# Attention matmuls cut into four column tiles, two jobs of VectorE handed to ScalarE and GpSimd, and a new hand-written order

## What is computed

```python
xn = _layernorm(x, axis=-1)
q, k, v = split_heads(xn @ W_q), split_heads(xn @ W_k), split_heads(xn @ W_v)
q, k = _apply_rope(q, cos, sin), _apply_rope(k, cos, sin)
scores = einsum('bhqd,bhkd->bhqk', q, k);  scores = where(causal, -inf, scores)
attn = softmax(scores / sqrt(hd), axis=-1)
s = einsum('bhqk,bhkd->bhqd', attn, v) ... @ W_o
g = _silu(_L0_ffn_ref(xn, w_router, w_fc, w_proj))
x = x + s * g
```

## Time and profile before

| | |
|---|---|
| median of three runs | 2545.77 us |
| the profiled execution | 2543.15 us |
| its span in the profile | 2541.4 us |
| TensorE matmul busy | 2411.2 us, 95% |
| TensorE weight loads busy | 1227.6 us, 48% |
| VectorE busy | 2100.8 us, 83% |
| ScalarE busy | 1732.6 us, 68% |
| GpSimd busy | 969.9 us, 38% |
| granted TensorE clock over the span | 0.981 |

### The profile page before, as it was taken

One profiled execution on the slowest core, in us unless ns is written; L12 is line 12 of the kernel. 1 busy time (PEld: TensorE's weight loads), 2 busy tenths in 40 slices (PEclk: granted clock), 3 DMA queues, 4 the chain that ended last, 5 costly groups with the idle time before them and its releaser, 6 DMA issues. The chain is left out here.

```text
span 2541.4 us, 51444 instructions
## 1 busy us (share of the span) xinstructions
PE 2411.2 (95%) x16364; PEld 1227.6 (48%) x16365; DVE 2100.8 (83%) x5995; ACT 1732.6 (68%) x4063; POOL 969.9 (38%) x1124
## 2 busy tenths in 40 slices
PE   7979985999999999999999999999999999899887
PEld 6767761334334334333333333333433433588676
DVE  7979988989989989988998998998998999355344
ACT  6767771777777777777777777777777777555211
POOL 6979994112122222222222222222222222222676
PEclk9999995999999999999999999999999999999999
DMA  6898977767755655655666665565565561498898
GB/s 223 276 282 284 294 260 141 156 159 147 153 93 94 116 97 90 114 102 96 104 107 128 102 110 94 99 110 100 93 106 106 92 104 44 141 311 312 266 370 273
DMA packets 302398, 403.44 MB, mean 159 GB/s; under 512 B 99248, under 2 KB 233648, under 8 KB 302000
## 3 DMA queue, kind: packets, MB, share of 16 engines
q1 hardware_dynamic: 289840, 366.58, 60.9%
q0 software_dynamic: 12288, 33.57, 4.9%
HBM read 225.46 MB, written 173.02 MB: 157 GB/s over the span
## 5 line engine op out<-in xcount | busy, mean ns | idle before, releaser
L945 DVE CUSTOM_DVE_ANT_0 dump<-ps_rows,mask 128x128 bf16<-128x128 f32 (+7 forms) x2048 | 1483.0, 755 | 171.0 <-issue 151.2
L924 ACT ACTIVATE probs<-ps_cols 128x512 f32<-128x512 f32 (+3 forms) x3072 | 1275.1, 505 | 471.6 <-PE ps_cols L1091 466.0
L1091 PE MATMUL ps_cols<-q_st,k_st 99*128 99x512 bf16 (+3 forms) x3072 | 835.6, 329 | 8.3 <-DMA q_st<-max_T 3.2
L903 POOL TENSOR_SCALAR_AFFINE_SELECT probs<-probs 128x512 f32<-128x512 f32 x512 | 325.3, 635 | 1284.9 <-ACT probs L924 1284.7
L1036 PE MATMUL ps_rows<-k_st,q_st 96*128 96x512 bf16 (+3 forms) x3072 | 776.2, 330 | 14.3 <-DVE row_max L945 6.8
L1068 PE MATMUL ps_ctx<-probs,v_st 128*32 128x512 f32 (+3 forms) x6144 | 615.5, 495 | 0.0
L1091 PEld LDWEIGHTS ps_cols<-q_st,k_st 99*128 99x128 bf16 x3072 | 274.0, 97 | 497.6 <-ACT probs L924 293.3
L1036 PEld LDWEIGHTS ps_rows<-k_st,q_st 96*128 96x128 bf16 x3072 | 279.2, 98 | 321.3 <-DVE row_max L945 168.1
L1068 PEld LDWEIGHTS ps_ctx<-probs,v_st 128*32 128x32 f32 x6144 | 140.3, 108 | 214.4 <-ACT probs L924 78.0
L945 DVE DVE_READ_ACCUMULATOR2_ANT row_max<- 128x1 f32 x2048 | 171.1, 84 | 0.2
L316 POOL TENSOR_TENSOR rest<-roped,parts 128x1024 f32<-128x1024 f32 x64 | 138.3, 2161 | 36.1 <-ACT parts L367 31.4
(11 more groups left out here) (114 smaller groups left out, 2458.6 us busy)
## 6 DMA issues: line engine op xcount, KB each, us to landing
parts_dram<-parts SPq DMA_DIRECT2D x64, 768.0 KB, 4.1
q_st<-parts_dram SPq DMA_DIRECT2D x384, 128.0 KB
k_st<-parts_dram SPq DMA_DIRECT2D x384, 128.0 KB
xs_dram<-zeros SPq DMA_DIRECT2D x36, 512.0 KB, 7.0
xs_sb<-xs_dram SPq DMA_DIRECT2D x72, 256.0 KB, 4.7
g_dram<-g_sb SPq DMA_DIRECT2D x72, 256.0 KB, 3.6
v_dram<-v_sb SPq DMA_DIRECT2D x32, 544.0 KB, 5.0
v_st<-v_dram SPq DMA_DIRECT2D x64, 272.0 KB
```

The source lines that it names most:

```text
L903: nc.gpsimd.affine_select(out=tri, in_=tri, compare_op=ALU.is_ge, fill=0.0, base=0, pattern=[[0, GH], [1, P]], channel_multiplier=-1).then ...
L924: nc.scalar.activation(probs[:, k % PB, h, 0:w], ps_cols[(GH * k + h) % CB][:, 0:w], ACT.Exp).then_inc(exp_done, 1)
L945: nc.vector.tensor_tensor_reduce(out=dump[:, even, 0:n], in0=ps_rows[:, 512 * bank:512 * bank + n], in1=mask[:, S - n:S], scale=1.0, scala ...
L1091: nc.tensor.matmul(ps_cols[(GH * k + h) % CB][:, 0:w], k_st[r][:, j // IB, h * 512 + (j % IB) * P:h * 512 + (j % IB + 1) * P], q_st[r][:, ...
```

## The change

1. Every matmul of the attention is issued in column tiles of 32. A row or column matmul of 128 stationary columns becomes four of 32 that stream the same moving operand. The transpose of maxima becomes two (32 and 16 columns). The transpose of contexts becomes plain fp32 matmuls against the 68 used columns of the identity, four tiles for each of four blocks. Only the last one of a set signals.
2. The maxima leave their bank by ScalarE (`move_max`). The contexts leave theirs by ScalarE too, into a new SBUF tile `ctx_T` (`move_ctx`). VectorE takes the reciprocals from there (`invert`), three row items later, and GpSimd multiplies (`normalise`), two steps after the transpose.
3. `slot_done` is split into `rows_done`, `max_moved`, `ctx_moved` and `normalised`. `place()` works out for each use of a bank which of them to wait for.
4. `ITEMS` and `ORDER` are new, SyncE loads the next group's maxima before it stores the contexts of half 0, and the first group's operands are loaded at tile 10 of the first phase in place of 8.

```diff
-    FIRST_GROUP_AT = 8
+    FIRST_GROUP_AT = 10
...
-        ("RR", "", "RRR", "VR"),
-        ("", "RM", "RX", ""),
-        ("RVR", "RR", "RR", ""),
-        ("R", "VR", "", ""),
-        ("R", "", "R", "VVR"),
-        ("", "", "R", "R"),
-        ("V", "R", "", "R"),
-        ("", "RV", "", "R"),
-        ("X", "M", "R", ""),
-        ("R", "", "RV", ""),
-        ("R", "R", "VV", ""),
-        ("RR", "", "", "VV"),
+        ("R", "RR", "RR", "VR"),
+        ("", "RRM", "RV", "R"),
+        ("", "RRX", "RR", ""),
+        ("VR", "", "R", "R"),
+        ("", "", "RV", "V"),
+        ("", "R", "RV", "R"),
+        ("", "R", "", "RV"),
+        ("R", "", "R", "V"),
+        ("R", "", "X", "MR"),
+        ("", "V", "R", ""),
+        ("R", "VR", "", "R"),
+        ("V", "", "", "RV"),
...
-            store_ctx(n, b, r, 0)
             if not last:
                 load_max(n + 1, (r + 1) % RING, 0)
+            store_ctx(n, b, r, 0)
...
+        def normalise(n, c):
+            pool.wait_ge(inv_ready, 2 * n + c + 1)
+            if n > 0:
+                pool.wait_ge(ctx_stored[c], 16 * n)
+            nc.gpsimd.tensor_tensor(ctx_out[:, c].rearrange("p i (h e) -> p (i h) e", h=GH), ctx_T[:, c, :, 0:HD],
+                                    inv_sum[:, c, :].unsqueeze(2).broadcast_to((P, IB * GH, HD)),
+                                    ALU.mult).then_inc(normalised, 1)
+
         def group(n, r, first, last):
             for k, (c, j, q0, w, diag_before, diag) in enumerate(STEPS):
+                for k0, _, (what, arg) in in_group(n):
+                    if what == "ctx" and k == min(k0 + 2, NS - 1):
+                        normalise(n - arg, arg)
...
+        def move_max(n, c, slot, bank):
+            act.wait_ge(slot_ready, slot + 1)
+            if n > 0:
+                act.wait_ge(max_loaded[c], 16 * n)
+            nc.scalar.activation(max_T[:, c, :], small_bank(bank)[0:PARTS * GH * IB, 0:P],
+                                 ACT.Copy).then_inc(max_moved, 1)
+
+        def move_ctx(n, c, slot, bank):
+            act.wait_ge(slot_ready, slot + 1)
+            if n > 0:
+                act.wait_ge(normalised, 2 * (n - 1) + c + 1)
+            nc.scalar.activation(ctx_T[:, c].rearrange("p i e -> p (i e)"),
+                                 ps_rows[:, 512 * bank:512 * bank + IB * GH * VP], ACT.Copy).then_inc(ctx_moved, 1)
...
-        def copy_max(m, c, slot, bank):
-
-            if not (isinstance(m, int) and m == 0):
-                dve.wait_ge(max_loaded[c], 16 * m)
-            dve.wait_ge(slot_ready, slot + 1)
-            nc.vector.tensor_copy(max_T[:, c, :], small_bank(bank)[0:PARTS * GH * IB, 0:P])\
-                .then_inc(slot_done, 1)
...
+        def invert(m, c):
+            dve.wait_ge(ctx_moved, 2 * m + c + 1)
+            if m > 0:
+                dve.wait_ge(normalised, 2 * (m - 1) + c + 1)
+            nc.vector.reciprocal(inv_sum[:, c, :], ctx_T[:, c, :, HD]).then_inc(inv_ready, 1)
...
-                mm = nc.tensor.matmul(ps_rows[:, 512 * (bank + c):512 * (bank + c) + w], q,
-                                      k_st[r][0:KS, c, h * 512:h * 512 + w], start=True, stop=True)
+                for a in range(0, P, VW):
+                    mm = nc.tensor.matmul(ps_rows[a:a + VW, 512 * (bank + c):512 * (bank + c) + w],
+                                          q_st[r][0:KS, i // IB, q0 + a:q0 + a + VW],
+                                          k_st[r][0:KS, c, h * 512:h * 512 + w], start=True, stop=True,
+                                          tile_position=(0, a))
...
+            for a in range(0, PARTS * GH * IB, VW):
+                b = min(a + VW, PARTS * GH * IB)
+                mm = nc.tensor.transpose(small_bank(bank)[a:b, 0:P], parts[:, a:b], ident_b[:], tile_position=(0, a))
...
+            used = ident_f[:].rearrange("p (h e) -> p h e", h=GH)[:, :, 0:VP]
             for i in range(IB):
-                mm = nc.tensor.transpose(ps_rows[:, 512 * bank + i * P:512 * bank + (i + 1) * P],
-                                         ctx_raw[:, c, i * P:(i + 1) * P], ident_f[:])
+                at = 512 * bank + i * GH * VP
+                for a in range(0, P, VW):
+                    mm = nc.tensor.matmul(ps_rows[a:a + VW, at:at + GH * VP].rearrange("p (h e) -> p h e", h=GH),
+                                          ctx_raw[:, c, i * P + a:i * P + a + VW], used, start=True, stop=True,
+                                          tile_position=(0, a))
...
+                    k0 = h * 512 + (j % IB) * P
+                    for a in range(0, P, VW):
+                        mm = nc.tensor.matmul(ps_cols[(GH * k + h) % CB][a:a + VW, 0:w],
+                                              k_st[r][:, j // IB, k0 + a:k0 + a + VW],
+                                              q_st[r][:, c, h * 512 + q0 - 512 * c:(h + 1) * 512],
+                                              start=True, stop=True, tile_position=(0, a))
```

More of the change, by code:

```diff
@@ L711, in attention_phase, with in_group, happens @@
     EVENTS = events()
[L712 to L734, removed]
-    def place():
[L739 to L743, removed]
+    assert not any(x in "MX" for x in ORDER[-1][-1])
+    def in_group(n):
+        return [(k, h, what) for k, h, what in EVENTS if what[0] != "values" and happens(what, n)]
+    def happens(what, n):
+        return not (n == 0 and what in (("ctx", 1), ("values", -1)) or
+                    n == N - 1 and (what[0] == "row" or what == ("max", 0)))
+    def place():
+        uses = [[("row", t) for t in range(NI)] + [("max", 0)]] + \
+               [[what for _, _, what in in_group(n)] for n in range(N)] + [[("ctx", 1)]]
+        out, last, number = [], {}, 0
+        left = {"row": 0, "max": 0, "ctx": 0}
+        for whats in uses:
+            pos, placed = 0, {}
             for what in whats:
@@ L747, in place, with moves_after, rows_before_inverse @@
                 banks = [(pos + i) % RB for i in range(2 if wide else 1)]
-                last_use = max(used.get(x, -1) for x in banks)
-                placed.append((banks[0], at - last_use if last_use >= 0 else None))
-                used.update({x: at for x in banks})
+                before = {"row": 0, "max": 0, "ctx": 0}
+                for kind, count in [last[b] for b in banks if b in last]:
+                    before[kind] = max(before[kind], count)
+                left[what[0]] += 1
+                last.update({b: (what[0], left[what[0]]) for b in banks})
+                placed[what] = (number, banks[0], before)
                 pos += len(banks)
-                at += 1
+                number += 1
             out.append(placed)
[L754 to L764, removed]
+        return out
+    FIRST_ROWS, *PLACES = place()
     def small_bank(i):
         return ps_rows[:, 512 * i:512 * (i + 1)].bitcast(BF16)
-    assert PER % 2 == 0 and (GH * NS) % CB == 0 and NS % PB == 0
+    def moves_after(n, k, h):
+        k0, h0 = (k, h - 1) if h > 0 else (k - 1, GH - 1)
+        return [what for kk, hh, what in in_group(n) if (kk, hh) == (k0, h0) and what[0] != "row"]
+    INVERT_AFTER = 3
+    def rows_before_inverse(n):
+        out, rows, due = {}, 0, {}
+        place_of = [(k, h) for k, h, _ in in_group(n)]
+        for i, (k, h, what) in enumerate(in_group(n)):
+            if what[0] == "row":
+                rows += 1
+            elif what[0] == "ctx":
+                same = sum(1 for x, y in zip(place_of[i + 1:], in_group(n)[i + 1:]) if x == (k, h) and y[2][0] == "row")
+                out[what] = min(rows + same + INVERT_AFTER, NI)
+        return out
+    assert (GH * NS) % CB == 0 and NS % PB == 0
     def groups(eng, body):
@@ L999, in group @@
             if last:
                 for i in range(MAX_OPS):
[L1001 to L1017 removed]
+                    split_max(n, 1, i)
+            else:
+                for t in range(NI):
+                    row_item(n + 1, t, *PLACES[n]["row", t][:2])
+                    if t < MAX_OPS:
+                        split_max(n, 1, t)
+                    if HALF_ITEMS <= t < HALF_ITEMS + MAX_OPS:
+                        split_max(n + 1, 0, t - HALF_ITEMS)
+                    for (_, c), rows in inverses.items():
+                        if rows == t + 1:
+                            invert(n - c, c)
@@ L1019, in _, with banks_free @@
+            if last:
+                for _, c in inverses:
+                    invert(n - c, c)
         groups(dve, group)
-        last_slot = base(N - 1) + len(slots(False, True))
-        normalise(N - 1, 1, last_slot, 0)
+        invert(N - 1, 1)
     @block.tensor
     def _(pe):
-        def banks_free(slot, distance):
-            if distance is not None:
-                pe.wait_ge(slot_done, slot - distance + 1)
-        def row_item(r, t, slot, bank, distance):
+        def banks_free(before):
+            if before["row"]:
+                pe.wait_ge(rows_done, before["row"])
+            if before["max"]:
```

(3 more changed lines are left out.)

138 lines of the change are left out of this document (51 added, 87 removed), and 6 rows, old and new, of the table ITEMS.

## The result

The changed kernel takes 2450.17 us (median of four runs, 2448.09 to 2453.28), the kernel before 2545.35 beside it: a ratio of 0.963, 95% interval 0.961 to 0.964. The forecast was 2414 us in a range of 2365 to 2505. The direction and the mechanism held; a quarter of the forecast gain was missing.

What follows compares the result with a forecast made beforehand. TensorE was taken as the attention's bound, at 98% of each 27.41 us group. Its new work of 24.40 us plus 0.9 gives 25.3: -133 us over 63 groups, +1 at the tail, so 2414 us, range 2365 to 2505.

Steps and rivals of the forecast that it cites:

- the lower bound that I took: In TensorE's attention matmuls, four 32-column bfloat16 tiles take 0.216 us per 512 columns, like one full matmul.
- rival 2: TensorE's narrow sets are bound by 108 ns weight loads: 1.6 us more, 26.9 us per group, 2515 us; chance 0.1.
- rival 4: Gaps around the value blocks aren't due to tile shape and stay: 27.4 us per group, 2546 us; chance 0.05.
- the sum's last term, the waits: Per attention group, 0.9 us of waits on top of TensorE's 24.40 us, since VectorE and ScalarE have less slack.
- Rival 1: TensorE's 1096 instructions a group come too slowly: gain ends at 25 ns each, 43 ns gives 3790 us; chance 0.08.

Runs made afterwards that it cites:

- Tiles alone: The kernel before with only its four matmul sites in column tiles; order, banks, VectorE's copies and product kept: 2512 us, ratio 0.988.
- paced: The changed kernel with each group's 13 operand-load DMAs issued piece by piece after the steps of values, not in one burst: 2424 us, ratio 0.953.

## Why the prediction held, and where it was off

The bound was read right. TensorE's own distances between starts showed the shape changes, and they are gone: 0.44 us for two row sets, then the values at once. The pace of bfloat16 tiles is the lower bound that I took; rival 2 (narrow sets bound by loads) is refuted by 0.06 us between sets of 128 columns, rival 4 by the missing gaps. The Trainium skill, "TensorEngine Tiling (Array Packing)", Key Properties, says that a change of the tiling mode drains TensorE and a change of the tile alone does not; the traces agree, as far as 32 against 128 and 48 columns go: about 0.1 us at each change before, and 0.06 us from one set of four tiles to the next now.

The group without a stall came out at 25.29 for 25.3. That it did so to 0.01 us is luck: the 0.9 us of waits in it were a choice between 0.6 and 2.3 that no row decided. Of the moved jobs GpSimd's product took 622 ns for 0.7 us, ScalarE's moves 276 and 391 to 433 ns for 276 and some 390. VectorE's 23.39 us were forecast as 23.53.

The step that failed is the sum's last term, the waits. I put 0.9 us there for VectorE and ScalarE, which covers the group without a stall, and nothing for TensorE's instructions. The changed kernel's groups have 0.65 us more on average, 40 us in all, which covers the distance from 2414 to 2450. The 17 gaps hold some 25 of these 40 us and the stretch at the lower clock up to 3.4; the rest I haven't taken apart. Pacing the loads and spreading the weights takes the mean to 25.37 us and the kernel to 2418. Rival 1 looked at the right resource with the wrong question: it asked for the time of one instruction, 25 ns, on an even supply. The supply isn't even. It comes in packets of 256, and what counts is whether one packet's delay, up to some 6.5 us from the request, fits into the time in which TensorE goes through one. Before, that was some 17 us, and delays of up to 9 us left no gap; now it is 5.9 (median).

A second step was right by its sum and wrong in its reasons. I booked the whole gain to the tiles and the new tables at nothing. Tiles alone bring 32 of the 95 us. The new tables are written for kernels without shape changes (12 blocks of values where the old had nine), and with the moved jobs. Without the tiles the kernel is slower than before (2631 us, part of it the fp32 matmul at full width); with the tiles but without the moved jobs they bring nothing that is clear of noise. A sum of engine times does not see this: in the tiled kernel with the old tables the moved jobs take 1.3 us from VectorE, and the group grows from 26.05 to 26.73 us, because TensorE waits for ScalarE to empty the bank of the maxima.

Open: what sets the 4% on the slower chips; what stops ScalarE every third group in the kernel with tiles and new tables; and how far the moved jobs would pay with tables made for them and no tiles, which wasn't tried.

## What to carry to other kernels

Look between the starts of matmuls, not at busy time, where operands of different widths alternate: here each change of tile shape cost about 0.1 us, 22 of them a group. When an edit multiplies an engine's instructions, ask how long a DMA burst keeps the rings full and compare that with the time the engine takes for 256 instructions, and spread the bursts. A hole of 2 to 3 us can cost more than its length, because TensorE's clock may be at the lower level behind it. A hand-written order is part of the kernel it was made for: judge it together with the edits, not alone.

## What the runs showed of the hardware

TensorE's instructions come through the same DMA engines as the data, in 16 KB packets that take 0.9 to 1.9 us, 1.1 in the median. In all 17 long gaps of the changed kernel TensorE went on 1.2 to 1.7 us after such a packet's end, and with 13 loads of 1.8 MB in the rings a packet started up to some 6.5 us after its request, by the count above. A set of four 32-column bfloat16 tiles costs what one 128-column matmul costs, down to 128 moving columns (0.055 to 0.058 us), and four tiles of 16 moving columns take 0.029 us. Behind some holes of TensorE its granted clock was 0.50: for 6.8 us behind 2.2 us (changed) and 3.0 us (paced), for 3.4 us behind five gaps of 2.2 to 2.5 us in tiles alone. Behind the changed kernel's gap of 2.5 us at 1228.18 it was not.
